# Six-point short convolution: the taps counted from an offset of two, so that the point zero has four taps instead of five

## The reference

```python
xc = jnp.transpose(x, (0, 2, 1))
h = _bn(_conv1d(xc, conv1_w, 0), bn1_g, bn1_b, bn1_m, bn1_v)   # 1 tap, 128 -> 128 channels
h = jax.nn.relu(h)
h = _bn(_conv1d(h, conv2_w, 8), bn2_g, bn2_b, bn2_m, bn2_v)    # 17 taps, padding 8
x_conv = jnp.transpose(jax.nn.relu(h + xc), (0, 2, 1))
...
msg = jax.nn.relu(x @ w_msg.T + b_msg)
x_nmp = jnp.einsum('bnm,bmd->bnd', A, msg)                     # A = exp(-dist) * adj
gi = x_in @ w_ih.T + b_ih ; gh = x @ w_hh.T + b_hh             # a gated unit, then layer norm
...
h = relu(((1 + eps) * x + adj @ x) @ W1 + b1) @ W2 + b2        # second layer, then layer norm
```

## Time and profile before

| | before |
|---|---|
| median of 3 runs | 396.47 us |
| the profiled execution, its own time | 396.53 us |
| its span, first to last instruction | 394.7 us |
| PE busy | 366.0 us, 93% |
| DVE busy | 318.2 us, 81% |
| ACT busy | 230.8 us, 58% |
| POOL busy | 226.1 us, 57% |
| mean granted clock of PE | 0.982 |

### The profile page before, as it was taken

The page is one execution under the profiler, slowest core; times in us unless marked ns, Lnnn a source line. Parts: engine busy times, 40 slices in busy tenths (PEclk is TensorE's granted clock), DMA queues, the critical chain, the costliest instruction groups (busy, mean ns, idle before and its releaser), DMA issues.

```text
span 394.7 us, 6487 instructions
## 1 busy us (share of the span) xinstructions
PE 366.0 (93%) x2191; PEld 319.3 (81%) x2191; DVE 318.2 (81%) x669; ACT 230.8 (58%) x423; POOL 226.1 (57%) x195
## 2 busy tenths in 40 slices
PE   2969795999999999999999999999999999999974
PEld 1848784979888898979888898979988898988954
DVE  4899879599588986999688986999778976986564
ACT  3535454373676567673676567574675557472773
POOL 3659362298437863497437963397436963395343
PEclk9999898799999999999999999999999999999998
DMA  6500000430101300120101201130101301000011
GB/s 231 216 0 1 2 2 1 159 109 1 55 4 49 108 29 27 55 106 0 53 0 53 106 14 39 53 106 2 53 2 53 108 2 55 1 2 0 2 53 53
DMA packets 7991, 19.39 MB, mean 49 GB/s; under 512 B 672, under 2 KB 5024, under 8 KB 6944
## 3 DMA queue, kind: packets, MB, share of 16 engines
q1 hardware_dynamic: 7536, 18.50, 13.4%
q10 hardware_dynamic: 432, 0.59, 0.4%
HBM read 14.90 MB, written 4.19 MB: 48 GB/s over the span
## 4 chain that ended last, share of the span: by engine, by line
PE 79%; DVE 12%; issue 3%; ACT 3%; DMA 2%; POOL 1%; SPq 0%; DVEq 0%; ACTq 0%; POOLq 0%
PE conv L1218 25%; PE back L1218 23%; PE front L1316 7%; PE back L1316 7%; PE back L1405 6%; DVE xl L821 5%; PE front L1288 2%; PE conv L1266 2%; PE back L1367 2%; DMA tail<-in_conv_dram 2%; PE front L1308 1%; ACT nmph L615 1%; PE conv L1288 1%; PE front L1298 1%; DVE wl L1042 1%
## 5 line engine op out<-in xcount | busy, mean ns | idle before, releaser
L1218 PE MATMUL conv<-sth,wh 128*128 128x256 f32 x238 | 74.6, 313 | 7.2 <-DVE wl L1042 4.6
L1218 PE MATMUL conv<-stl,wh 128*128 128x256 f32 x238 | 69.3, 291 | 0.0
L1218 PE MATMUL conv<-sth,wl 128*128 128x256 f32 x238 | 69.1, 290 | 0.0
L516 POOL TENSOR_TENSOR rstd<-rstd,minus_half 128x4 f32<-128x4 f32 (+1 forms) x34 | 38.8, 1141 | 38.2 <-DVE rstd L993 37.6
L1218 PEld LDWEIGHTS conv<-sth,wh 128*128 128x128 f32 x238 | 46.6, 196 | 11.2 <-DVE wl L1042 4.8
L521 POOL TENSOR_TENSOR xw<-xw,xv 128x512 f32<-128x512 f32 (+1 forms) x17 | 20.9, 1230 | 52.0 <-ACT xw L681 52.0
L534 POOL TENSOR_TENSOR amat<-amat,adjT 128x512 f32<-128x512 f32 x32 | 49.4, 1577 | 1.4 <-ACT amat L657 1.4
L1218 PEld LDWEIGHTS conv<-stl,wh 128*128 128x128 f32 x238 | 46.7, 196 | 0.3
L1218 PEld LDWEIGHTS conv<-sth,wl 128*128 128x128 f32 x238 | 46.5, 195 | 0.0
L615 ACT ACTIVATE sth<-sv 128x272 fp32r<-128x272 f32 (+1 forms) x35 | 18.2, 519 | 41.3 <-DVE sv L840 26.9
L528 POOL TENSOR_TENSOR tail<-xn,later_w 128x512 f32<-128x512 f32 (+1 forms) x17 | 29.8, 1756 | 4.3 <-DMA out_dram<-tail 2.6
(11 more groups left out here) (219 smaller groups left out, 1010.9 us busy)
## 6 DMA issues: line engine op xcount, KB each, us to landing
adjT<-in_adj_dram SPq DMA_DIRECT2D x8, 1024.0 KB, 4.8
out_dram<-tail SPq DMA_DIRECT2D x15, 256.0 KB, 2.2
xv<-in_x_dram SPq DMA_DIRECT2D x7, 512.0 KB, 3.3
gbuf<-in_gates_dram SPq DMA_DIRECT2D x1, 576.0 KB, 6.5
tail<-in_conv_dram ACTq DMA_DIRECT2D x2, 256.0 KB, 3.8
xv<-in_x_dram SPq DMA_DIRECT2D x2, 256.0 KB, 4.8
later_w<-in_later_dram SPq DMA_DIRECT2D x1, 452.0 KB, 6.9
tail<-in_conv_dram SPq DMA_DIRECT2D x1, 320.0 KB, 5.4
```

The lines of the kernel that those rows point to most:

```text
L516: done(pool.tensor_tensor(rstd[:, k, h, q], rstd[:, k, h, q], minus_half[:, q], ALU.pow), RSTD[k])
L1218: ins = pe.matmul(bank, a, b, start=first and k == 0, stop=last and k == len(todo) - 1)
```

## The change

Two slots of zeros are put ahead of the 17 taps and one behind, so there are 20 slots, five for each of the four coefficients. Coefficient 0 then holds (nothing, tap 2, 6, 10, 14), coefficient 1 (nothing, 3, 7, 11, 15), coefficient 2 the taps 0, 4, 8, 12, 16, and coefficient 3 the taps 1, 5, 9, 13 and nothing. `ZERO` skips its empty first slot and has four taps, `INF` four, the others five: 33 in all. The input is turned to match: even and odd halves of a quad change places in `h1`, the second of them one quad later, which `h1_out` does with two ACTIVATEs of 128x256 instead of one of 128x512. The sums of DVE and POOL run over five slots (640 elements), ACT's copies of tap 16 go, and POOL zeroes the added slots by two memsets at its start.

```diff
-NTAP = (5, 5, 5, 5, 5, 5, 4)
+LEAD, PLACES = 2, 5
+NTAP = (5, 4, 5, 5, 5, 5, 4)
...
-        c2raw = tail[:, 0:TAPS * P].rearrange("p (k o) -> p k o", k=TAPS)
+        padded = tail[:, 0:4 * PLACES * P].rearrange("p (k o) -> p k o", o=P)
+        c2raw = padded[:, LEAD:LEAD + TAPS, :]
+        coef = [padded[:, j:4 * PLACES:4, :] for j in range(4)]
...
                 pool.memset(minus_half[:, :], -0.5).then_inc(exponent_set, 1)
+                pool.memset(padded[:, 0:LEAD, :], 0.0).then_inc(ends_zeroed, 1)
+                pool.memset(padded[:, LEAD + TAPS:, :], 0.0).then_inc(ends_zeroed, 1)
...
-                pool.tensor_tensor(ataps[:, 10:14, :], c2raw[:, 0:16:4, :], c2raw[:, 2:16:4, :],
-                                   ALU.add).then_inc(tap_sums_one, 1)
+                pool.tensor_tensor(ataps[:, 10:15, :], coef[0], coef[2], ALU.add).then_inc(tap_sums_one, 1)
...
-                done(act.activation(h1[:, 2 * h:2 * h + 2, :, :, PAD:PAD + TQ].rearrange("p b r q m -> p (b r) q m"),
-                                    conv1_bank(h, ahead)[:, :].rearrange("p (c m q) -> p c q m", c=GB, q=2), ACT.Relu,
-                                    bias=bn[:, 2:3], scale=bn[:, 0:1]), H1_READY)
+                src = conv1_bank(h, ahead)[:, :].rearrange("p (c m q) -> p c q m", c=GB, q=2)
+                for q in range(2):
+                    rows_q = h1[:, 2 * h:2 * h + 2, :, 1 - q, PAD + q:PAD + q + TQ].rearrange("p b r m -> p (b r) m")
+                    last = act.activation(rows_q, src[:, :, q, :], ACT.Relu, bias=bn[:, 2:3], scale=bn[:, 0:1])
+                done(last, H1_READY)
...
                 act.wait_ge(conv2_loaded, 64)
-                last_tap = c2raw[:, TAPS - 1:TAPS, :]
-                act.activation(gtaps[:, 4:15:5, :], last_tap.to_broadcast([P, 3, P]), ACT.Copy).then_inc(tap_copies, 1)
-                act.activation(ataps[:, 4:10:5, :], last_tap.to_broadcast([P, 2, P]), ACT.Copy).then_inc(tap_copies, 1)
...
-                dve.scalar_tensor_tensor(gtaps[:, 10:14, :], w3, 0.5, w2, ALU.mult, ALU.add).then_inc(tap_sums, 1)
+                dve.scalar_tensor_tensor(gtaps[:, 10:15, :], w3, 0.5, w2, ALU.mult, ALU.add).then_inc(tap_sums, 1)
...
-                taps_step(ataps[:, 5:9, :], ataps[:, 5:9, :], -2.0, utaps[:, 0:4, :])
+                taps_step(ataps[:, 5:10, :], ataps[:, 5:10, :], -2.0, utaps[:, 0:5, :])
```

More of the change, by code:

```diff
@@ L190, in gnn_kernel @@
         utaps = usum[:, :, :, :].rearrange("p b r t -> p (b r t)").rearrange("p (k o) -> p k o", o=P)
-        traw = (gtaps[:, 10:15, :], c2raw[:, 0:TAPS:4, :], gtaps[:, 5:10, :], ataps[:, 5:10, :],
-                gtaps[:, 0:5, :], ataps[:, 0:5, :], c2raw[:, 3:TAPS:4, :])
+        traw = (gtaps[:, 10:15, :], coef[0][:, 1:5, :], gtaps[:, 5:10, :], ataps[:, 5:10, :],
+                gtaps[:, 0:5, :], ataps[:, 0:5, :], coef[3][:, 0:4, :])
         W_ORDER = ("conv1", HALF, ZERO, PLUS2, PLUS1, "gates", "w1", MINUS2, MINUS1, INF)
@@ L314, in gnn_kernel @@
         tap_sums_one = sem("tap_sums_one")
-        tap_copies = sem("tap_copies")
+        ends_zeroed = sem("ends_zeroed")
         def wait(eng, name, g, j):
@@ L557, in prologue @@
                 streams2(0)
+                pool.wait_ge(ends_zeroed, 2)
                 pool.wait_ge(conv2_loaded, 64)
-                pool.tensor_tensor(ataps[:, 10:14, :], c2raw[:, 0:16:4, :], c2raw[:, 2:16:4, :],
-                                   ALU.add).then_inc(tap_sums_one, 1)
-                pool.tensor_tensor(ataps[:, 0:4, :], c2raw[:, 1:16:4, :], c2raw[:, 3:16:4, :],
-                                   ALU.add).then_inc(tap_sums_one, 1)
+                pool.tensor_tensor(ataps[:, 10:15, :], coef[0], coef[2], ALU.add).then_inc(tap_sums_one, 1)
+                pool.tensor_tensor(ataps[:, 0:5, :], coef[1], coef[3], ALU.add).then_inc(tap_sums_one, 1)
                 pool.wait_ge(tap_sums_one, 2)
-                pool.tensor_tensor(gtaps[:, 0:4, :], ataps[:, 10:14, :], ataps[:, 0:4, :], ALU.add).then_inc(tap_sums_one, 1)
+                pool.tensor_tensor(gtaps[:, 0:5, :], ataps[:, 10:15, :], ataps[:, 0:5, :], ALU.add).then_inc(tap_sums_one, 1)
                 pool.wait_ge(tap_sums_one, 3)
-                pool.tensor_tensor(ataps[:, 0:4, :], ataps[:, 10:14, :], ataps[:, 0:4, :],
+                pool.tensor_tensor(ataps[:, 0:5, :], ataps[:, 10:15, :], ataps[:, 0:5, :],
                                    ALU.subtract).then_inc(tap_sums_one, 1)
@@ L728, in prologue @@
                 h1_out(0, 1)
-                act.wait_ge(tap_copies, 2)
                 act.wait_ge(tap_sums, 3)
@@ L1076, in prologue @@
                 dve.tensor_copy(gbias[:, 3:4], vec[:, BIH + 2:BIH + 3]).then_inc(bn_ready, 1)
+                dve.wait_ge(ends_zeroed, 2)
                 dve.wait_ge(conv2_loaded, 64)
-                w0, w1, w2, w3 = (c2raw[:, k:16:4, :] for k in range(4))
+                w0, w1, w2, w3 = coef
                 steps = [0]
@@ L1084, in taps_step @@
                     dve.scalar_tensor_tensor(out, a, scale, b, ALU.mult, ALU.add).then_inc(tap_sums, 1)
-                dve.scalar_tensor_tensor(gtaps[:, 10:14, :], w3, 0.5, w2, ALU.mult, ALU.add).then_inc(tap_sums, 1)
+                dve.scalar_tensor_tensor(gtaps[:, 10:15, :], w3, 0.5, w2, ALU.mult, ALU.add).then_inc(tap_sums, 1)
                 steps[0] += 1
-                taps_step(gtaps[:, 10:14, :], gtaps[:, 10:14, :], 0.5, w1)
-                taps_step(gtaps[:, 10:14, :], gtaps[:, 10:14, :], 0.5, w0)
+                taps_step(gtaps[:, 10:15, :], gtaps[:, 10:15, :], 0.5, w1)
+                taps_step(gtaps[:, 10:15, :], gtaps[:, 10:15, :], 0.5, w0)
                 first_diffs()
@@ L1093, in prologue @@
                 parts2(0)
-                taps_step(utaps[:, 0:4, :], w2, 4.0, w0)
-                taps_step(ataps[:, 5:9, :], w3, 4.0, w1)
-                taps_step(gtaps[:, 5:9, :], ataps[:, 5:9, :], 2.0, utaps[:, 0:4, :])
+                taps_step(utaps[:, 0:5, :], w2, 4.0, w0)
+                taps_step(ataps[:, 5:10, :], w3, 4.0, w1)
+                taps_step(gtaps[:, 5:10, :], ataps[:, 5:10, :], 2.0, utaps[:, 0:5, :])
                 dve.wait_ge(later_loaded, 16)
@@ L1226, in taps @@
                 k1 = NTAP[n] if k1 is None else k1
+                at = 1 if n == ZERO else 0
                 if k0 == 0:
@@ L1238, in taps @@
                 for k in range(k0, k1):
-                    ins = products(conv_out(n), [weights(n, k) + (sth[:, n, :, k:k + TQ], stl[:, n, :, k:k + TQ])],
+                    ins = products(conv_out(n), [weights(n, k) + (sth[:, n, :, at + k:at + k + TQ],
+                                                               stl[:, n, :, at + k:at + k + TQ])],
                                    first=k == 0, last=k == NTAP[n] - 1)
@@ L1248, in first_taps @@
                     wait(pe, E_READY_H, 0, 1)
-                    pe.wait_ge(tap_copies, 2)
                     pe.wait_ge(tap_sums, 3)
@@ L1265, in first_taps @@
                 for k in range(NTAP[n]):
-                    ins = pe.matmul(conv_out(n), traw[n][:, k, :], sv[:, ROW[n], :, k:k + TQ], start=k == 0,
+                    at = k + 1 if n == ZERO else k
+                    ins = pe.matmul(conv_out(n), traw[n][:, k, :], sv[:, ROW[n], :, at:at + TQ], start=k == 0,
                                     stop=k == NTAP[n] - 1)
```

## The result

| | before | after |
|---|---|---|
| median of 14 runs each | 396.46 us | 397.98 us |
| lowest and highest | 395.86, 398.39 | 397.22, 398.67 |
| profiled execution, its own time | 396.53 | 397.73 |
| its span | 394.7 | 395.9 |
| ratio of the runs, 95% interval | 1 | 1.0029 (1.0016 to 1.0041) |

The changed kernel is slower: by 1.5 us (0.38%) by the medians, and by 0.29% by the ratio, which is that of the means (396.74 and 397.90 us). The ratio is just under the bound of 0.3% named in the prediction, and its interval lies above 1 throughout; the median is over the 397.66 us that the prediction named as slower. The prediction was 396.65 with a range of 394.8 to 398.0.

A forecast was written before the change was run, and what follows sets the result against it. The prediction took PE's number of columns to bound the alike rounds. From 396.53 us it took 2.55 for the rounds, added 1.97 for the prologue and 0.7 for the clock: 396.65 us, range 394.8 to 398.0.

The forecast's parts named there:

- PE in the rounds: ZERO loses three matmuls of 256 columns, 0.365 us a round; over seven rounds 2.55 us less.
- everything carried over has slack: In the rounds, PLUS2's low stream is ready 1.0 us early; 0.4 us stays after shorter ZERO and split write.
- The split write: Writing h1 by two ACTIVATEs costs +0.22 us a pair, hidden by slack, so nothing in the rounds.
- The prologue's sum: Longer DVE and POOL sums, taking turns, delay MINUS2 and the first round by 1.97 us; bounds 0.8 and 2.2.
- the rival without turns: In the prologue DVE and POOL grow only by their own elements, +0.8 us, no added slow stretch: 394.8 us, chance 0.20.
- The clock: A longer PE hole ahead of the prologue's MINUS2 brings half clock; 0.7 us taken between 0 and +2.16.
- the slower rival: The prologue's added half-clock stretch costs its full 2.16 us, giving 398.1 us; chance 0.17.
- the swap: The prologue's new slow stretch replaces the one after the 2.65 us hole ahead of the first round, summing to 0.
- The forecast of no change: Whole kernel's time stays within 0.3%, 1.19 us, between 395.28 and 397.66 us; chance 0.54.
- The near cancellation: Gains in the rounds and losses in the prologue nearly cancel: 396.65 us, within about 395.5 to 397.6, chance 0.55.
- the rival with the slow stretch in full: Half clock in the prologue costs 2.16 us besides the 1.97 of longer sums: 398.1 us, chance 0.17.
- Both of its signs: Clock at 0.50 at 26 to 30 us and also at the first round's start; prologue then loses 4.1 us.

## Why the prediction was right where it was, and what it mis-sized

**PE in the rounds: right, but six times, not seven.** 0.37 us a round by the chain, and the run with five taps at ZERO gives 2.4 us back. The first round returned 0.03 in the profile. There the 0.36 gained by its first 42 matmuls was lost to a slow stretch that took more time (6.14 us for the 30 matmuls instead of 5.80), and with the clock held full its PLUS2 waits for the stream. The prediction's argument that everything carried over has slack used a row of an alike round; the first round, which comes out of the prologue with its streams late, has none.

**The split write: right.** 1.02 us a pair instead of 0.78, no wait of PE at PLUS2 in the rounds, and 44.71 us a round in the run with the split alone. In the prologue it is about 0.24 us where the write of `h1` comes last, which the prediction had only in its upper bound; the time of that run doesn't exclude up to 1.3 us.

**The prologue's sum: right in size.** +0.37 for the first three sums (0.36 predicted), +1.61 for the rest (0.40 + 1.08 + 0.13), 1.98 in all against 1.97. The first of the two isn't isolated by any run: the write of `h1` ended with the third sum in the two traces, and in other executions it came last. POOL's part alone is 1.19 by the run with four slots (1.08 predicted), and the turns themselves are shown by the run with POOL held back. The rule that the Trainium skill gives in "SBUF — State Buffer", section "SBUF: two separate sides", an exclusive lock for a whole instruction, agrees with the rows: line 913 took 1.61 us beside POOL's 1.53. Told by the rows alone: the rival without turns, 394.8, is out.

**The clock: the term that was mis-sized.** I set 0.7 us. In the profile MINUS2 lost 2.18 us to half clock behind the hole of 4.57, and only 0.17 of it was absorbed on the way to the first round; nor was the stretch ahead of the first round spared in return. The row of the longest hole, 2.16, which I had given to the slower rival, was the right one for this execution. The later holes are nearly unchanged in length (2.4 us for 2.6, and 4.6 in both) and kept their slow stretches, so the swap that I had counted on in part didn't come. Against the median the term is smaller than against the profile, since the kernel before loses time behind its holes too. With the holes filled the changed kernel gains 4.5 us by its ratio (1.0029 to 0.9916) and the one before 3.5 (1 to 0.9913). At full clock the two are equal (+0.06 us by the medians, within about 0.6), where the prediction's terms without the clock give 1.97 - 2.55 = -0.58: the first round's missing 0.36 is part of that, and the rest is inside the spread. So what the two kernels differ by, 1.1 us by the ratio and 1.5 by the medians, is the clock's, give or take 0.6, where 0.7 was set.

**The forecast of no change** holds by the ratio alone, 1.0029 where the bound was 1.003; by the medians the change is slower, 397.98 where the bound was 397.66. That it came out on this side is luck. The near cancellation, 395.5 to 397.6, to which the prediction gave 0.55, is not what happened; what happened is the rival with the slow stretch in full, 398.1, to which it gave 0.17. Both of its signs came: the clock was 0.50 from 26 us on and again at the start of the first round, and the prologue lost 1.98 + 2.16 = 4.1 us. The time is inside the range and near its top, where that rival stood.

## What to carry to other kernels

A change that shortens the steady rounds has to be priced where the operands are made ready too: here eleven instructions grew by a quarter, most of them on the one chain that TensorE waited for, and since VectorE and GpSimd took turns, both engines' growth was added. A longer wait of TensorE can be paid twice, once as the wait and once in the matmuls behind it at half clock; matmuls that nothing reads, put into such a hole, made both kernels faster (393.9 us, 0.992 and 0.991 of before). When times of one kernel spread over 2 to 3 us, look at the granted clock of more than one profile before comparing single executions.

## What the hardware showed unexpectedly

The length of TensorE's pause alone did not decide whether the clock fell to 1.2 GHz. After a pause of 3.20 us it stayed at 2.4 GHz in one execution and after one of 3.21 at the same place it fell in another. A pause of 2.42 us was followed by half clock, and so were pairs of pauses of 2.59 and 1.78 and of 1.24 and 1.78; one of 3.49 was not. The clock can fall inside the pause (at 22.9 us in the changed kernel's trace, where PE stood still until 25.19) or after matmuls have begun again (at 42.8 us in the trace of before, 0.6 us after they did). A fall cost 1.3 us (MINUS2 3.74 instead of 2.44) to 2.5 us (30 matmuls 6.14 instead of 3.64) of matmul time in these runs.

A VectorE operation of 24 elements takes 0.19 us alone, 0.88 beside a GpSimd operation of 512 elements and 1.41 beside one of 640: it ends within 0.05 us of its neighbour's end (20.27 and 20.22 us before, 21.02 and 20.97 after), so what it takes is what is left of that one.
